# Linear layer: the two feed-forward products as three fp32r products each, and attention outputs turned into the keys' place

## The chip, the cores and the metric

The kernel runs on one core of one Trainium2 chip. The time is the device time of one execution in microseconds (us); a figure for a kernel is the median of several executions. A smaller time is better.

## The reference, cut to what matters

The program has four sublayers on an input of 8 x 1024 tokens with 256 features: softmax attention, a small linear map, a block with linear attention and a feed-forward part, and a mixture of experts. The change is in the third. What it computes (cut):

```python
x = x + _linear_attention(_layernorm(x, ln1_g, ln1_b), Wq, Wk, Wv, Wo)
h = _layernorm(x, ln2_g, ln2_b)
x = x + jax.nn.gelu(h @ Wf1, approximate=False) @ Wf2
```

`Wf1` is 256 x 1024 and `Wf2` is 1024 x 256, both in float32. These two products, over all 8192 tokens, are the feed-forward products of the title.

## The kernel before, in words

`linear_layer` walks over 16 groups of 512 tokens (8 batches, two groups each). The first group and the last are written out, and the 14 between run in a hardware loop whose body holds two. Each engine (TensorE PE, VectorE DVE, ScalarE ACT, GpSimd POOL, and SP for DMAs) has its own stream of instructions written out by hand in this order; the engines meet only at semaphores. Nothing is scheduled: what is written first on an engine runs first.

PE does in a group, in this order: queries and keys (`QK`, 16 results of 128 x 512), transposes of the keys (`KT`), the chunks of linear attention (`score`, and products into `psum_n` and `psum_u`), the transposes of its outputs (`turn_o`), the transposes of the next group's normalized input, the output product (`two_tiles` with `wo`), the next group's values (`next_v`), the transposes of the second norm's result (`turn` with `U["T2"]`), the first feed-forward product F1 (`by_feature`, L1367), and the second, F2 (`two_tiles` with `wf2`, L1377). All of these use a ring of three PSUM banks, `l_general`: a unit of work waits until the bank that it takes was emptied.

Queries, keys and values are already made in the way that the change brings to the feed-forward part: both operands are split into a high part rounded to fp32r and a low part, what is left of it, and three fp32r products (high with high, high with low, low with high) are added up in PSUM (`split_product`, L1415). The experts sublayer does the same for both of its products (L2223 and L2238). F1, F2 and the output product take plain float32 operands. A float32 matmul stands as two records in the trace, an fp32r matmul as one.

Around F1 and F2: ACT empties the two transposed tiles with scale and shift into `l_nT2` (`turned`, L1579); PE waits for both and makes F1's eight tiles of 128 features; ACT applies Gelu to each (L1645) and writes it into the place of the queries (`hT = qT`); PE waits for the last of these, then makes F2's two units, and DVE adds each to `a3` (`add_a3`, L1906). Next PE goes on to the following group's `QK`, or, behind the last group, to the remaining small steps.

Before the first group, SP loads all weights; DVE makes the high parts of `Wq`, `Wk`, `Wv` (`high_weights`, L1995 and L1999) and POOL the low parts (`low_weights`, L1728). The differences that DVE needs on the way lie in `oT`, which is not yet in use.

## Time and profile before

| | us |
|---|---|
| median of 3 runs | 4660.64 |
| lowest and highest run | 4648.56, 4662.6 |
| the profiled execution's own time | 4661.58 |
| its span in the trace | 4659.8 |

| engine | busy us | share of the span |
|---|---|---|
| PE (matmul) | 4148.9 | 89% |
| PEld (weight loads, beside PE) | 3068.7 | 66% |
| DVE | 2640.0 | 57% |
| ACT | 1911.6 | 41% |
| POOL | 1179.2 | 25% |

The shares are means over stages with different limits, so they only say where to look. The linear layer runs from about 1460 to 3700 us of the span, and PE is busy nearly all through it. A matmul's record begins when it starts and ends when its last result is out, and the next one may start before that end; the pace of a stream of matmuls is therefore read from start to start, not from the length of a record.

### The profile page before, as it was taken

How to read it: one execution, taken by the hardware profiler on the slowest of the kernel's cores; microseconds unless marked ns; L12 is line 12 of the kernel's file. 1: busy time of each engine (PE TensorE's matmuls, PEld its weight loads, DVE VectorE, ACT ScalarE, POOL GpSimd, SP SyncE). 2: the span in 40 equal slices, each digit the busy share in tenths (PEclk: the TensorE clock that was granted, in tenths of full speed). 3: DMA queues.
4: the chain of work that ended last, by engine and by line, in shares of the span. 5: the costliest groups of instructions: out<-in, count | busy, mean ns of one | idle time of the engine just before them, and what ended most of it. 6: DMA issues, size and time to landing. Idle time of an engine off the chain costs nothing. (4 is left out here: it accounts for less than half of the span.)

```text
span 4659.8 us, 76082 instructions
## 1 busy us (share of the span) xinstructions
PE 4148.9 (89%) x26100; PEld 3068.7 (66%) x26100; DVE 2640.0 (57%) x7848; ACT 1911.6 (41%) x3047; POOL 1179.2 (25%) x1094
## 2 busy tenths in 40 slices
PE   5999999999983999999999999999999499999990
PEld 2444444444432787777777877777787398989890
DVE  4787887788843455544445544444554265555554
ACT  1566666566652333333323333332333133333222
POOL 3233433334323011111111111111111123333334
PEclk8999999999976999999999999999999699999995
DMA  4443353344312000000000000000000123333335
GB/s 74 80 88 56 73 110 85 61 80 83 65 49 74 1 19 19 15 14 19 13 11 15 15 15 11 15 12 5 13 13 9 58 60 61 65 60 67 60 65 199
DMA packets 168246, 222.18 MB, mean 48 GB/s; under 512 B 26732, under 2 KB 143435, under 8 KB 167872
## 3 DMA queue, kind: packets, MB, share of 16 engines
q1 hardware_dynamic: 139840, 180.74, 16.8%
q0 software_dynamic: 25728, 28.03, 3.9%
q10 hardware_dynamic: 2304, 8.39, 0.4%
q8 instruction: 238, 3.90, 0.4%
q14 instruction: 136, 1.11, 0.1%
HBM read 85.92 MB, written 86.65 MB: 37 GB/s over the span
## 5 line engine op out<-in xcount | busy, mean ns | idle before, releaser
L787 ACT ACTIVATE probs<-a_scores 128x1024 f32<-128x1024 f32 (+3 forms) x768 | 615.8, 812 | 369.7 <-PE a_scores L691 363.1
L948 DVE CUSTOM_DVE_ANT_0 a_scores<-a_scores,mask 128x384 f32<-128x384 f32 (+3 forms) x1024 | 482.0, 515 | 119.8 <-PE a_scores L677 113.9
L1906 DVE TENSOR_TENSOR l_a<-l_general,l_a 128x512 f32<-128x512 f32 x64 | 44.3, 692 | 736.0 <-PE l_general L1377 736.0
L691 PEld LDWEIGHTS a_scores<-q_st,k_st 50*128 50x128 f32 x1536 | 150.1, 192 | 407.7 <-issue 275.6
L252 POOL TENSOR_TENSOR l_ln_rstd<-l_ln_ve,minus_half 128x4 f32<-128x4 f32 x80 | 84.1, 1051 | 1308.7 <-DVE l_ln_ve L225 1308.4
L691 PE MATMUL a_scores<-q_st,k_st 50*128 50x512 f32 (+3 forms) x1536 | 351.9, 456 | 34.2 <-issue 25.2
L951 DVE TENSOR_REDUCE mx<-a_scores 128x2 f32<-128x1024 f32 x256 | 310.7, 1223 | 110.8 <-PE a_scores L677 109.5
L711 PE MATMUL a_out<-probs,v_aug 128*32 128x512 f32 (+3 forms) x3072 | 347.6, 526 | 3.0 <-POOL probs L880 2.9
L677 PE MATMUL a_scores<-k_st,q_st 48*128 48x512 f32 (+3 forms) x1536 | 308.7, 400 | 45.6 <-ACT probs L787 27.7
L2307 POOL DMA_INDIRECT expert_sums_scratch<-e_y,e_number x136 | 220.2, 1619 | 369.0 <-DMA expert_sums_scratch<-e_y,e_number 317.0
L2238 PE MATMUL e_out<-e_weights_lo,e_hT_hi 128*128 128x256 f32 x1088 | 307.9, 283 | 0.0
L2238 PE MATMUL e_out<-e_weights_hi,e_hT_lo 128*128 128x256 f32 x1088 | 307.6, 283 | 0.0
L2238 PE MATMUL e_out<-e_weights_hi,e_hT_hi 128*128 128x256 f32 x1088 | 307.2, 282 | 0.0
L880 POOL TENSOR_SCALAR_AFFINE_SELECT probs<-probs 128x512 f32<-128x512 f32 x256 | 163.3, 639 | 560.1 <-ACT probs L787 556.6
L1517 PE MATMUL l_num<-l_v,l_scores_kept 128*128 128x65 f32 x2048 | 285.4, 262 | 0.0
L2285 ACT ACTIVATE e_to_split<-e_hidden,e_b 128x384 f32<-128x384 f32 (+1 forms) x320 | 200.0, 625 | 202.7 <-PE e_hidden L2223 197.1
L1517 PEld LDWEIGHTS l_num<-l_v,l_scores_kept 128*128 128x128 f32 x2048 | 270.3, 192 | 0.0
L1613 ACT ACTIVATE l_o<-l_general 128x512 f32<-128x512 f32 x256 | 152.9, 597 | 268.5 <-PE l_general L1415 246.1
L1367 PE MATMUL l_general<-l_nT,l_wf 128*128 128x512 f32 x512 | 225.5, 599 | 18.9 <-ACT l_nT L1579 18.9
L2223 PE MATMUL e_hidden<-e_rT_hi,e_weights_hi 128*128 128x384 f32 (+1 forms) x640 | 236.0, 369 | 0.0
L1377 PE MATMUL l_general<-l_wf,l_qT 128*128 128x256 f32 x1024 | 225.2, 381 | 11.4 <-ACT l_qT L1645 11.4
L2223 PE MATMUL e_hidden<-e_rT_lo,e_weights_hi 128*128 128x384 f32 (+1 forms) x640 | 232.6, 363 | 0.0
(243 smaller groups left out, 9538.7 us busy)
## 6 DMA issues: line engine op xcount, KB each, us to landing
q_st<-parts SPq DMA_DIRECT2D x192, 128.0 KB, 4.6
k_st<-parts SPq DMA_DIRECT2D x192, 128.0 KB, 6.3
expert_rows_scratch<-empty_row SPq DMA_DIRECT2D x8, 2210.0 KB, 14.4
e_weights<-in_L_ffn_W_dram SPq DMA_DIRECT2D x16, 1024.0 KB, 8.2
e_rows<-expert_rows_scratch SPq DMA_DIRECT2D x24, 390.0 KB
e_rows<-expert_rows_scratch SPq DMA_DIRECT2D x16, 520.0 KB
x_in<-in_L_attn_x_dram SPq DMA_DIRECT2D x8, 1024.0 KB, 6.3
expert_sums_scratch<-empty_row SPq DMA_DIRECT2D x8, 1024.0 KB, 16.4
```

Of the source, the lines that this page charges most:

```text
L677: last = nc.tensor.matmul(psum_r[:, R.slot(u), h2, 0:w], q_st[rows, 2 * hg + pair, j * P:(j + 1) * P], k_st[rows, 2 * hg + pair, k0:k1], s ...
L691: last = nc.tensor.matmul(psum_r[:, R.slot(u), h2, 0:w], k_st[rows, 2 * hg + pair, i * P:(i + 1) * P], q_st[rows, 2 * hg + pair, q0:q0 + w ...
L711: last = nc.tensor.matmul(psum_o[32 * h4:32 * h4 + 32, q0 - half * HALF:HALF], v_aug[:, i, h * DV0:h * DV0 + 32], probs[:, k % 3, h4, 0:w] ...
L787: nc.scalar.activation(probs[:, k % 3, 2 * pair:2 * pair + 2, 0:w], psum_r[:, R.slot(u), :, 0:w], ACT.Exp).then_inc(R.evacuated[R.slot(u)], 1)
L948: last = nc.vector.tensor_tensor_reduce(s, s, mask[:, HALF - w:HALF], 1.0, LEAST, ALU.add, ALU.max, out[:, h2, :])
L951: last = nc.vector.tensor_reduce(out.rearrange("p h a -> p (h a)"), psum_r[:, R.slot(u), :, 0:w], AX.X, ALU.max)
L1367: last = nc.tensor.matmul(psum_g[:, G.slot(u), :], w[:, c, cols], nT[:, c, :], start=(c == 0), stop=(c == CD - 1))
L1377: last = nc.tensor.matmul(psum_g[:, G.slot(u), jj * D:(jj + 1) * D], lhs[:, k, j * P:(j + 1) * P], rhs[:, k, :], start=(k == 0), stop=(k = ...
L1517: last = nc.tensor.matmul(psum_n[:, NUM.slot(n), h4 * DV:(h4 + 1) * DV], scores[:, d % 2, h2, p % 4, :], v_aug[:, j, 4 * g4 + h4, :], star ...
L2223: last = nc.tensor.matmul(psum_h[:, HU.slot(u), 0:n * P], w1[a][:, e2, c, m * P:(m + 1) * P], rT[b][:, q % 2, c, 0:n * P], start=(k == 0), ...
L2238: last = nc.tensor.matmul(psum_y[:, s, (j - 2 * s) * D:(j - 2 * s + 1) * D], hT[a][:, q % 2, m, j * P:(j + 1) * P], w2[b][:, e2, m, :], st ...
L2307: nc.gpsimd.indirect_dma_start(out=sums_dram, out_offset=bass.IndirectOffsetOnAxis(ap=number[:, q % RING, j:j + 1], axis=0), in_=y[:, q % ...
```

## The change

Weights. `wf1` and `wf2` become pairs of a high and a low part in fp32r. The float32 weights are loaded into the place of `kt` (`raw_f`); before the first group DVE casts both to their high parts, and POOL, behind its other low parts, subtracts to get the low ones. In the first group, ACT waits for all four before its first copy into `kt`, and PE before F1. The low parts' places also hold the differences that lay in `oT` before.

Activations. ACT writes `turned2` (the result of the second norm, turned) and `hidden` (the Gelu's results, a ring of four tiles) into the place of `kt`. DVE casts each tile to its high part and subtracts to get its low part, in the places of `l_nT2`, the queries and the keys. `oT` is no longer a tile of its own but the place of `kT`, so ACT writes the turned attention outputs where the keys were.

PE. F1's tile is six fp32r products over 512 columns (before: two float32 matmuls), F2's token tile is 24 fp32r products over 256 columns (before: eight float32 matmuls). PE waits for the high parts of the activations before F1's first product and for the low ones before its fifth; in F2, waits for hidden tile m stand in the first token tile only, one before each third product. The former waits for ACT before F1 and F2 are gone. A semaphore on POOL is merged into another.

```diff
+                def by_feature(g, u, m):
+                    cols = slice(m * P, (m + 1) * P)
                     G.wait_free(pe, g, u)
+                    terms = [(c, a, "hi") for c in range(CD) for a in ("hi", "lo")]
+                    terms += [(c, "hi", "lo") for c in range(CD)]
+                    for k, (c, a, b) in enumerate(terms):
+                        if m == 0 and k == 0:
+                            pe.wait_ge(split_hi, g * NSPLIT + CD)
+                        if m == 0 and k == 2 * CD:
+                            pe.wait_ge(split_lo, g * NSPLIT + CD)
+                        last = nc.tensor.matmul(psum_g[:, G.slot(u), :], wf1[a][:, c, cols],
+                                                nT2_parts[b][:, c, :], start=(k == 0),
+                                                stop=(k == len(terms) - 1))
+                    last.then_inc(G.full[G.slot(u)], 1)
+
+                def feed_out(g, u, i):
+                    G.wait_free(pe, g, u)
+                    for jj in range(2):
+                        j = 2 * i + jj
+                        terms = [(m, a, b) for m in range(MF)
+                                 for a, b in (("hi", "hi"), ("hi", "lo"), ("lo", "hi"))]
+                        for k, (m, a, b) in enumerate(terms):
+                            if j == 0 and k % 3 == 0:
+                                pe.wait_ge(split_lo, g * NSPLIT + CD + m + 1)
+                            last = nc.tensor.matmul(psum_g[:, G.slot(u), jj * D:(jj + 1) * D],
+                                                    hT[a][:, m, j * P:(j + 1) * P], wf2[b][:, m, :],
+                                                    start=(k == 0), stop=(k == len(terms) - 1))
+                    last.then_inc(G.full[G.slot(u)], 1)
...
-                    for c in range(CD):
-                        G.wait_evacuated(pe, g, U["T2"] + c)
+                    if first:
+                        pe.wait_ge(f_weights, 4)
                     for m in range(MF):
-                        by_feature(g, U["F1"] + m, wf1, slice(m * P, (m + 1) * P), nT2)
-                    for u in range(U["F2"] - R, U["F2"]):
-                        G.wait_evacuated(pe, g, u)
+                        by_feature(g, U["F1"] + m, m)
                     for i in range(2):
-                        two_tiles(g, U["F2"] + i, i, hT, wf2, MF)
+                        feed_out(g, U["F2"] + i, i)
...
-                    turned(g, U["T2"], nT2, 2)
+                    turned(g, U["T2"], turned2, 2)
                     for m in range(MF):
                         u = U["F1"] + m
+                        if m >= TMP:
+                            act.wait_ge(split_lo, g * NSPLIT + CD + m - TMP + 1)
                         G.wait_full(act, g, u)
-                        nc.scalar.activation(hT[:, m, :], psum_g[:, G.slot(u), :],
+                        nc.scalar.activation(hidden[:, m % TMP, :], psum_g[:, G.slot(u), :],
                                              ACT.Gelu).then_inc(G.evacuated[G.slot(u)], 1)
...
                     last.then_inc(norm2_ready, 1)
+                    for c in range(CD):
+                        G.wait_evacuated(dve, g, U["T2"] + c)
+                        nc.vector.tensor_copy(nT2_hi[:, c, :], turned2[:, c, :]).then_inc(split_hi, 1)
+                    for c in range(CD):
+                        dve.wait_ge(split_hi, g * NSPLIT + c + 1)
+                        nc.vector.tensor_tensor(nT2_parts["lo"][:, c, :], turned2[:, c, :],
+                                                nT2_hi[:, c, :].bitcast(F32),
+                                                ALU.subtract).then_inc(split_lo, 1)
+                    for m in range(MF + 1):
+                        if m < MF:
+                            G.wait_evacuated(dve, g, U["F1"] + m)
+                            nc.vector.tensor_copy(hT["hi"][:, m, :], hidden[:, m % TMP, :]
+                                                  ).then_inc(split_hi, 1)
+                        if m > 0:
+                            dve.wait_ge(split_hi, g * NSPLIT + CD + m)
+                            nc.vector.tensor_tensor(hT["lo"][:, m - 1, :], hidden[:, (m - 1) % TMP, :],
+                                                    hT["hi"][:, m - 1, :].bitcast(F32), ALU.subtract).then_inc(split_lo, 1)
                     add_a3(g, s, U["F2"])
...
+                for n, w in enumerate((wf1, wf2)):
+                    pool.wait_ge(f_weights, 2)
+                    nc.gpsimd.tensor_tensor(w["lo"][:, :, :], raw_f[n], w["hi"][:, :, :].bitcast(F32),
+                                            ALU.subtract).then_inc(f_weights, 1)
...
+                dve.wait_ge(load, 64)
+                for n, w in enumerate((wf1, wf2)):
+                    nc.vector.tensor_copy(w["hi"][:, :, :], raw_f[n]).then_inc(f_weights, 1)
```

On PE, in the loop's first group, from the transposes of the second norm's result to the first product of the next group. `l_wf1` and `l_wf2` are the weights, `l_nT2` the turned norm, `l_qT` the place of the hidden tiles, a REGISTER_ALU or ISA row sets the count of a wait. Before:

```order
L1359 MATMUL l_general<-ident,l_norm 128x128 x8
L78 REGISTER_ALU
L1367 MATMUL l_general<-l_nT2,l_wf1 128x512 x8
L72 REGISTER_ALU
L1367 MATMUL l_general<-l_nT2,l_wf1 128x512 x6
...
L78 REGISTER_ALU
L1377 MATMUL l_general<-l_wf2,l_qT 128x256 x32
L72 ISA
L1415 MATMUL l_general<-l_nT1_hi,l_w_qkv_hi 128x512
```

The same place now; each of F1's eight tiles has the six products of the first, and behind the first two groups of three that are shown, F2 has 30 more:

```order
L1379 MATMUL l_general<-ident,l_norm 128x128 x8
L1390 ISA
L1393 MATMUL l_general<-l_nT2_hi,l_wf1_hi 128x512
L1393 MATMUL l_general<-l_nT2_hi,l_wf1_lo 128x512
...
L1393 MATMUL l_general<-l_nT2_lo,l_wf1_hi 128x512 x2
...
L1407 REGISTER_ALU
L1408 MATMUL l_general<-l_wf2_hi,l_hT_hi 128x256
L1408 MATMUL l_general<-l_wf2_lo,l_hT_hi 128x256
L1408 MATMUL l_general<-l_wf2_hi,l_hT_lo 128x256
L1407 REGISTER_ALU
L1408 MATMUL l_general<-l_wf2_hi,l_hT_hi 128x256
```

F1 grew from 16 matmuls to 48 and F2 from 32 to 96, at the same place between the transposes and the next group; nothing else of PE changed its place.

On DVE, at the same place, between the second norm (L268) and the addition of F2's result. Before:

```order
L225 TENSOR_TENSOR l_ln2_ve<-l_ln2_stats 128x4
L268 TENSOR_SCALAR l_norm<-l_a3,l_ln2_mean,l_ln2_rstd 128x256 x4
L75 REGISTER_ALU
L1906 TENSOR_TENSOR l_a3<-l_general,l_a3 128x512 x2
L78 REGISTER_ALU
```

Now (`l_k` is the place where ACT leaves the tiles to be split; six more pairs of a cast and a subtraction follow the last row shown before the "..."):

```order
L268 TENSOR_SCALAR l_norm<-l_a3,l_ln2_mean,l_ln2_rstd 128x256 x4
L78 REGISTER_ALU
L2043 CAST l_nT2_hi<-l_k 128x512 x2
L2045 ISA
L2046 TENSOR_TENSOR l_nT2_lo<-l_k,l_nT2_hi 128x512
...
L2052 CAST l_hT_hi<-l_k 128x512
L78 REGISTER_ALU
L2052 CAST l_hT_hi<-l_k 128x512
L2055 REGISTER_ALU
L2056 TENSOR_TENSOR l_hT_lo<-l_k,l_hT_hi 128x512
...
L1956 TENSOR_TENSOR l_a3<-l_general,l_a3 128x512 x2
```

Twenty DVE instructions came in here in each group, ten casts and ten subtractions, all ahead of the additions; the low part of a hidden tile stands behind the high part of the next tile.

## Rows read from the trace of the kernel before

**Rows 1.** The page: busy us, share, instructions; then the granted clock in 40 slices.

```profile
PE 4148.9 (89%) x26100; PEld 3068.7 (66%) x26100; DVE 2640.0 (57%) x7848; ACT 1911.6 (41%) x3047; POOL 1179.2 (25%) x1094
...
PEclk8999999999976999999999999999999699999995
```

**Rows 2.** Windows: stretch, its us, busy of PE, PEld, DVE, ACT, POOL, clock, DMA.

```profile
1772.00:1905.00 133.00, 126.59 (x791) 104.27 (x791) 64.38 (x216) 47.86 (x81) 20.67 (x19) 1.00 0.05 17
```

**Rows 3.** Timeline of PE around F1 and F2: start us, us, instruction, idle before.

```profile
1741.87 1.03 PE L1359 MATMUL l_general<-ident,l_norm 128*128 128x128 f32 x8
1744.11 13.97 PE L1367 MATMUL l_general<-l_nT,l_wf 128*128 128x512 f32 x32 [1.20 <-ACT l_nT L1579]
1758.77 14.08 PE L1377 MATMUL l_general<-l_wf,l_qT 128*128 128x256 f32 x64 [0.69 <-ACT l_qT L1645]
1772.50 0.58 PE L1415 MATMUL l_general<-l_nT_hi,l_w_qkv_hi 128*128 128x512 f32 x1
```

**Rows 4.** F1's line, L1367: count, ns min/median/max, first and last start.

```profile
L1367 PE MATMUL l_general<-l_nT,l_wf x512: 592/592/1192, 1609.5 to 3640.8; 128*128 128x512 f32 x171
```

**Rows 5.** Timeline of PE: first, second and last of the 48 products of `next_v`.

```profile
1730.45 0.58 PE L1415 MATMUL l_general<-l_w_qkv_hi,l_nT_hi 128*128 128x512 f32 x1
1730.87 0.39 PE L1415 MATMUL l_general<-l_w_qkv_lo,l_nT_hi 128*128 128x512 f32 x1
...
1741.64 0.40 PE L1415 MATMUL l_general<-l_w_qkv_hi,l_nT_lo 128*128 128x512 f32 x1
```

**Rows 6.** Timelines of PE and PEld in the experts' second product (42 products between).

```profile
3999.81 0.28 PE L2238 MATMUL e_out<-e_weights_hi,e_hT_hi 128*128 128x256 f32 x1
...
4004.85 1.04 PE L2205 MATMUL e_turned<-ident,e_rows 128*128 128x128 f32 x8
...
3999.81 0.19 PEld L2238 LDWEIGHTS e_out<-e_weights_lo,e_hT_hi 128*128 128x128 f32 x1
```

**Rows 7.** Timelines of ACT and DVE beside F1 and F2.

```profile
1742.56 1.45 ACT L1579 ACTIVATE l_nT<-l_general,l_affine 128x512 f32<-128x512 f32 x2
...
1758.12 0.60 ACT L1645 ACTIVATE l_qT<-l_general 128x512 f32<-128x512 f32 x1 [1.12 <-PE l_general L1367]
...
1765.98 0.69 DVE L1906 TENSOR_TENSOR l_a<-l_general,l_a 128x512 f32<-128x512 f32 x1 [28.94 <-PE l_general L1377]
```

**Rows 8.** Timelines of DVE and POOL: hidden tiles split in the experts sublayer.

```profile
4027.36 0.43 DVE L2326 CAST e_hT_hi<-e_to_split 128x512 fp32r<-128x512 f32 x1 [0.86 <-ACT e_to_split L2285]
4027.70 0.69 DVE L2347 TENSOR_TENSOR e_hT_lo<-e_to_split,e_hT_hi 128x512 fp32r<-128x512 f32 x1
4028.75 0.43 DVE L2326 CAST e_hT_hi<-e_to_split 128x512 fp32r<-128x512 f32 x1 [0.36 <-ACT e_to_split L2285]
...
4030.49 2.56 DVE L2347 TENSOR_TENSOR e_hT_lo<-e_to_split,e_hT_hi 128x512 fp32r<-128x512 f32 x2
...
4030.69 1.81 POOL L2300 TENSOR_TENSOR e_y<-e_y,e_gate 128x768 f32<-128x768 f32 x1 [3.91 <-DMA expert_sums_scratch<-e_y,e_number]
```

**Rows 9.** Timeline of POOL: the next group's low parts, and its first work behind F2.

```profile
1720.53 2.49 POOL L1664 TENSOR_TENSOR l_nT_lo<-l_o,l_nT_hi 128x512 fp32r<-128x512 f32 x2 [3.60 <-DMA expert_rows_scratch<-l_rows,l_to]
...
1781.13 1.01 POOL L252 TENSOR_TENSOR l_ln_rstd<-l_ln_ve,minus_half 128x4 f32<-128x4 f32 x1 [45.20 <-DVE l_ln_ve L225]
```

**Rows 10.** Timelines of DVE, POOL, PE and ACT before and in the first group.

```profile
1492.77 2.28 DVE L1995 SCALAR_TENSOR_TENSOR l_kT<-l_kT 128x2048 f32<-128x2048 f32 x1
1495.08 6.57 DVE L1999 SCALAR_TENSOR_TENSOR l_w_qkv_hi<-l_kT 128x2048 fp32r<-128x2048 f32 x1
1501.73 4.57 POOL L1728 TENSOR_TENSOR l_w_qkv_lo<-l_kT,l_w_qkv_hi 128x2048 fp32r<-128x2048 f32 x1 [2.23 <-DVE l_w_qkv_hi L1999]
...
1506.36 0.50 PE L1415 MATMUL l_general<-l_nT_hi,l_w_qkv_hi 128*128 128x512 f32 x1 [1.69 <-POOL l_w_qkv_lo L1728]
...
1509.35 0.69 DVE L1936 SCALAR_TENSOR_TENSOR l_qT<-l_general,l_o 128x512 f32<-128x512 f32 x1 [7.70 <-ACT l_o L1617]
...
1533.04 1.56 ACT L1625 COPY l_k<-l_general 128x512 f32<-128x512 f32 x3 [2.72 <-PE l_general L1488]
```

More of the change, by code:

```diff
@@ L1165, in linear_layer, with sb_with @@
         w_qkv = {part: sb(f"l_w_qkv_{part}", [P, 3, CD, E1], F32R) for part in ("hi", "lo")}
+        def sb_with(name, shape, other_name, other_shape):
+            with nc.sbuf_tensor(other_name, other_shape, F32) as other:
+                pass
+            return sb(name, shape, F32R), other
         wo = sb("l_wo", [P, ME, D])
-        wf1 = sb("l_wf1", [P, CD, DF])
-        wf2 = sb("l_wf2", [P, MF, D])
+        wf1, wf2 = ({"hi": sb("l_wf1_hi", [P, CD, DF], F32R)}, {"hi": sb("l_wf2_hi", [P, MF, D], F32R)})
+        wf1["lo"], diff_v = sb_with("l_wf1_lo", [P, CD, DF], "l_w_v_diff", [P, NP // 2, HALF])
+        wf2["lo"], diff_q = sb_with("l_wf2_lo", [P, MF, D], "l_w_q_diff", [P, NP // 2, HALF])
         wg = sb("l_wg", [P, CD, E])
@@ L1181, in linear_layer @@
         sb("l_rows_end", [P, G4 * RW - CD * HALF])
-        nT2 = sb("l_nT2", [P, CD, HALF])
-        qT = sb("l_qT", [P, NP, HALF])
-        kT = sb("l_kT", [P, NP, HALF])
+        nT2_hi, nT2 = sb_with("l_nT2_hi", [P, CD, HALF], "l_nT2", [P, CD, HALF])
+        hT = {}
+        hT["hi"], qT = sb_with("l_hT_hi", [P, MF, HALF], "l_qT", [P, NP, HALF])
+        hT["lo"], kT = sb_with("l_hT_lo", [P, MF, HALF], "l_kT", [P, NP, HALF])
+        with nc.sbuf_tensor("l_nT2_lo", [P, CD, HALF], F32R) as nT2_lo:
+            pass
         kt = sb("l_k", [P, G4, E1])
@@ L1190, in linear_layer @@
         o = sb("l_o", [P, 2, E1])
-        oT = sb("l_oT", [P, ME, HALF])
-        hT = qT
+        oT = kT
+        flat_k = kt[:, :, :].rearrange("p j (a n) -> p (j a) n", n=HALF)
+        turned2, hidden = flat_k[:, 2:4, :], flat_k[:, 4:8, :]
+        TMP = 4
+        nT2_parts = {"hi": nT2_hi, "lo": nT2_lo}
         ex = o[:, :, :].rearrange("p s (a n) -> p (s a) n", n=HALF)
@@ L1269, in linear_layer @@
         scatter_begun = sem("l_scatter_begun")
-        rows_gone = sem("l_rows_gone")
+        f_weights = sem("l_f_weights_split")
+        split_hi, split_lo = sem("l_split_hi_ready"), sem("l_split_lo_ready")
+        NSPLIT = CD + MF
         x2_read = sem("l_x2_read")
@@ L1328, in _ @@
                                          allow_slow_non_contiguous=True).then_inc(raw_loaded[0], 16)
-                for dst, w in ((wo, Wo), (wf1, Wf1), (wf2, Wf2), (wg, Wg)):
-                    sp.dma_start(dst[:, :, :], w.rearrange("(c p) n -> p c n", p=P)).then_inc(load, 16)
+                for dst, w in ((wo[:, :, :], Wo), (raw_f[0], Wf1), (raw_f[1], Wf2), (wg[:, :, :], Wg)):
+                    sp.dma_start(dst, w.rearrange("(c p) n -> p c n", p=P)).then_inc(load, 16)
                 def store(g, s):
@@ L1620, in group @@
                         turned(g, U["T3"], nT2, None)
+                    if first:
+                        act.wait_ge(f_weights, 4)
                     for i in range(8):
@@ L1717, in group @@
                             pool.wait_ge(scattered[k], g * G4 * 16)
-                        pool.sem_inc(rows_gone, 1)
+                        pool.sem_inc(scatter_begun, 1)
                     if not last_group:
```

7 lines of the change are left out of this document (2 added, 5 removed).

## The prediction, made before the changed kernel ran

> **What bounds the kernel now.** I read the page's first part and its slices, then windows of one group of the linear layer, then the timeline of PE around the changed place, and then that of the engines which feed it. PE is busy 89% of the span, and through the linear layer at the full granted clock [rows 1]. In a group of 133.00 us PE is busy 126.59, DVE 64.38, ACT 47.86 and POOL 20.67 us, at a clock of 1.00 (2.4 GHz) [rows 2]. So PE's instruction stream sets the time, and what leaves it shortens the group if no other engine takes its place. The reader should see in the timeline that F1 begins at 1744.11, 1.20 us after the last transpose, released by ACT; F2 begins at 1758.77, after 0.69 us of waiting for the last Gelu; the next group's first product begins at 1772.50 [rows 3]. From F1's start to that product it is 28.39 us: 14.66 for F1 and the wait behind it, 13.73 for F2. F1's line has 512 records, 32 for each of 16 groups [rows 4], so this stretch comes 16 times.
>
> **PE's products.** Two of the kernel's own streams have the form of the new ones. F1's 48 products of 128 x 512 are of the form and number of the values' products: those start at 1730.45 and the next work starts at 1741.87 [rows 3, 5], 11.42 us for 48, with a slow first step (0.42 us, rows 5) in it, which F1 will have too. F2's 96 products of 128 x 256 have the form of the experts' second product: 42 of them from 3999.81 to 4004.85 [rows 6], 0.120 us each, so 11.52 us. A record of 0.28 us or a weight load of 0.19 us is longer than that pace, because they overlap [rows 6]; the pace is what PE pays. Plain float32 cost 14.66 and 13.73 with the wait; the new streams cost 11.42 and 11.52.
>
> **The wait for Gelu ahead of F2 goes.** F2 now waits tile by tile, and its first tiles were ready long before. What is late next are the last two tiles. Call F2's start S. F1's last product starts 0.23 us before S (11.42/48 = 0.24 us is the pace) and by its record of about 0.40 us [rows 5] ends at S + 0.17. Gelu takes 0.60 [rows 7], so until about S + 0.8. DVE then casts the tile (0.43, of which the next instruction waits only 0.34, from 4027.36 to 4027.70), subtracts for tile 6 and then for tile 7 (0.69 each, about 0.6 from start to start) [rows 8]: tile 6 is ready at about S + 1.9, tile 7 at S + 2.55. PE needs tile m at S + 0.36 m (three products of 0.120): S + 2.16 and S + 2.52. So F2 loses 0 to 0.1 us here. I take 0.1. Each of these waits could also slow the product behind it. The nearest price is the slow first step of a stream, 0.42 instead of 0.24 us [rows 5], about 0.19; eight of them are 1.5 us. That is the upper bound; I take none beyond the 0.1, since in the values' stream every unit has such a wait and 48 products still keep to 11.42 us with one slow step.
>
> **A longer way into F1.** ACT empties the two transposed tiles from 1742.56 to 1744.01 [rows 7], and PE began 0.10 us later. Now a cast of the second tile stands between: with 0.43 us and a semaphore's step of about 0.07, PE begins some 0.5 us later. The two low parts follow the cast at 0.34 us, and take 0.6 and 0.69; the second is ready 1.7 us after ACT's end. PE starts 0.6 after ACT's end and has four products that need no low part, 1.1 us with the slow first step, so it waits 0 to 0.1 there. Together 0.6 us. Bounds: 0.4 if the cast is all that is seen, 1.3 if both casts and both subtractions stand behind ACT's end in a row (2 x 0.43 + 2 x 0.69 = 2.24 us, less the 1.1 us of products that cover it, and the step of 0.1 to 0.2).
>
> **DVE and ACT through F1.** PE now makes a tile in 1.43 us (11.42/8). ACT needs 0.60. DVE needs a cast and a subtraction, 0.34 + 0.6 = 1.0 us, and in the experts sublayer, where it does just that at PE's pace, it sits idle 0.36 us per tile [rows 8]. DVE has 28.94 us free here [rows 7], and 20 instructions of 11 us in all fit; the additions behind them come due only when F2's first unit is done. ACT's ring of four tiles is given back by the subtraction two tiles later, well in time. What hides the split is thus that POOL is silent: in the experts, while POOL works on SBUF for 1.81 us, two subtractions take 2.56 [rows 8], 1.28 each. Here POOL has nothing to do from about 1736 to 1781 (45.20 us idle [rows 9]). The skill has the rule behind that row: the Trainium skill, "SBUF — State Buffer", section "Who interferes with whom", says that VectorE instructions with two SBUF inputs, and copies in the fast two-port mode, contend with GpSimd for one shared port pair, exclusively. By that rule the split would cost nothing in the loop and something before the first group, and both are as the rows say.
>
> **The group.** Before 28.39. After 0.6 + 11.42 + 11.52 + 0.1 = 23.64. Saved 4.75 us; 16 times, 76.0 us. With both upper bounds (1.3 and 1.5 for 0.6 and 0.1) it is 2.65 us a group, with both lower ones (0.4 and 0) 5.05: 42 to 81 us in all.
>
> **Attention outputs in the keys' place, the merged semaphore.** ACT's copies and PE's reads are the same in number, size and order; no wait is added. Zero.
>
> **Before the first group.** DVE casts two weights of 128 x 2048 behind 1501.65 (the end of its last high part), while POOL makes the last low part of `Wk` (4.57 us), which releases PE at 1506.36; DVE is next needed at 1509.35 [rows 10]. Nothing shows such a cast. Four times 0.34 is 1.4 us each, 2.7 for both, which fit the 7.70 us that DVE sits idle. But DVE's last high part took 6.57 us beside POOL's work where its neighbour without it took 2.28 [rows 10], so either of them may block the other. If the casts hold POOL up, PE starts up to 2.7 us later; if POOL holds the casts up until 1506.3, they end at 1509. I take 1 us, between 0 and 3. POOL's two new subtractions (4.6 us each, up to 6.6) end by 1523 and are wanted by ACT at 1533.04 [rows 10]: hidden by ten us of query and key products. The weights' DMAs keep their order.
>
> **The sum.** Profiled execution 4661.58 - 76.0 + 1 = 4586.6. The median of the runs is 4660.64, one us beside it; I do not correct for that. The runs lie between 4648.56 and 4662.6, so some 0.3% either way is noise, about what a measurement of this kernel can tell from no change.
>
> **The rivals.**
> *The waits inside F2 break its stream.* In the loop, each third product of the first token tile has a register instruction and a wait ahead of it, every 0.36 us, denser than any stream of products in the rows. At 0.19 us for each of eight, 1.5 us a group instead of 0.1: 22 us, so 4609. Against it stands the values' stream. It lies inside my range.
>
> *The weight loads set F2's pace, and the kernel is slower than before.* F2 goes from 64 records, each with a load, to 96. Its pace is 0.120 only if a load of 0.19 us lies beside other loads and products. If each product cost a load's 0.19 us instead, F2 would take 18.2 us, 6.7 more, and the group 30.3 instead of 28.39: 16 x 6.7 = 107, so 4694. The change loses from 0.17 us a product on ((28.39 - 0.6 - 11.42 - 0.1) / 96). Against it stand 42 products of exactly this form at 0.120 with loads of 0.19 beside them [rows 6]. The Trainium skill, "TensorE: Matmul & The Clock Gate", Part 3, "Packing small matmuls — row/col tiling", says that a weight load overlaps matmuls in flight only when their row groups differ; all these use all 128 rows. By that rule this rival would be the forecast. The trace disagrees with it, with 0.120 us between products whose loads take 0.19.
>
> *The gain is given back at a wait.* PE's next meeting with another engine could be late by as much as F2 is early, and the time stays at 4661. The one with a long chain is the low parts of the next group, behind POOL's scatter: they are ready at 1723.02 and used at 1730.45 [rows 5, 9], 7.4 us of slack, more than the 4.75 saved, and the chain starts in the same group's query stage, so it moves with PE. Little speaks for it.
>
> **How the numbers follow.** Forecast 4587, with the set-up and lead-in within their bounds, 0.82. Waits inside F2, 4609: 0.10. Weight loads, 4694: 0.04. Given back, 4661: 0.03. A mean gain larger than the bounds: 0.01. The range goes from 81 us of gain, less some noise, to beyond the second case: 4573 to 4612. Faster by over 0.3%: 0.93. Within 0.3%: 0.03. Slower: 0.04.
>
> **What would show it.** F1's products 0.23 to 0.24 us apart and F2's 0.120; from ACT's end to F1 0.6 us instead of 0.1; no wait of PE for Gelu; in F2 at most 0.1 us of waiting, at the seventh or eighth group of three; DVE idle between its pairs; a group of some 128 us. I would be wrong if F2's products stand 0.19 us apart, if F1's tiles come at DVE's pace, or if PE waits newly at the next group's low parts.

## The result and the profile after

The changed kernel takes 4605.98 us (median of 4 runs, 4591.81 to 4611.45), the kernel before 4661.62 us (4 runs, 4648.56 to 4673.35). The medians are 56 us apart. The ratio over all runs is 0.987, with a 95% interval from 0.9844 to 0.9896: 61 us less, between 48 and 73. Four more runs of the same kernel on another chip gave 4595.10 against 4661.07, a ratio of 0.9855 (0.984 to 0.9871), 66 us less by the medians. The prediction was 4587, 75 us less, with a range from 4573 to 4612. So the time lies inside the range, near its upper end, and some 10 to 20 us of the gain are missing.

The profiled execution after has 4610.1 us and a span of 4608.3. The page's busy times and granted clock after, answering to [rows 1]:

```profile
PE 4088.1 (89%) x26868; PEld 3115.5 (68%) x26868; DVE 2812.6 (61%) x8170; ACT 1910.7 (41%) x3047; POOL 1191.9 (26%) x1096
...
PEclk8899989999985999999999999999999699999995
```

PE has 61 us less to do and keeps its 89% of a shorter span; DVE has 173 us more and goes from 57 to 61%. One whole group of the loop after, from first query product to first query product (columns as in [rows 2]):

```profile
1650.71:1780.01 129.30, 123.38 (x848) 108.12 (x847) 75.39 (x236) 47.84 (x81) 21.76 (x20) 1.00 0.05 17
```

PE is still the engine without free time: 123.38 of 129.30 us. The changed place in that kernel, PE first, which answers to [rows 3] (start us, us, instruction, idle before and its releaser). Shown are the transposes, the first, second, fourth and fifth product of F1, the first two of F2, the first two of F2's eighth group of three, F2's last product and the next group's first:

```profile
1754.13 1.04 PE L1379 MATMUL l_general<-ident,l_norm 128*128 128x128 f32 x8
1756.78 0.50 PE L1393 MATMUL l_general<-l_nT_hi,l_wf_hi 128*128 128x512 f32 x1 [1.61 <-DVE l_nT_hi L2043]
1757.12 0.39 PE L1393 MATMUL l_general<-l_nT_hi,l_wf_lo 128*128 128x512 f32 x1
...
1757.58 0.40 PE L1393 MATMUL l_general<-l_nT_hi,l_wf_lo 128*128 128x512 f32 x1
1757.98 0.73 PE L1393 MATMUL l_general<-l_nT_lo,l_wf_hi 128*128 128x512 f32 x2
...
1768.39 0.28 PE L1408 MATMUL l_general<-l_wf_hi,l_hT_hi 128*128 128x256 f32 x1
1768.51 0.28 PE L1408 MATMUL l_general<-l_wf_lo,l_hT_hi 128*128 128x256 f32 x1
...
1770.91 0.39 PE L1408 MATMUL l_general<-l_wf_hi,l_hT_hi 128*128 128x256 f32 x1
1771.13 0.28 PE L1408 MATMUL l_general<-l_wf_lo,l_hT_hi 128*128 128x256 f32 x1
...
1779.90 0.28 PE L1408 MATMUL l_general<-l_wf_hi,l_hT_lo 128*128 128x256 f32 x1
1780.01 0.40 PE L1457 MATMUL l_general<-l_nT_hi,l_w_qkv_hi 128*128 128x512 f32 x1
```

DVE, ACT and PEld beside it:

```profile
1756.30 0.43 DVE L2043 CAST l_nT_hi<-l_k 128x512 fp32r<-128x512 f32 x1 [0.24 <-ACT l_k L1619]
1756.64 1.29 DVE L2046 TENSOR_TENSOR l_nT_lo<-l_k,l_nT_hi 128x512 fp32r<-128x512 f32 x2
...
1763.60 0.43 DVE L2052 CAST l_hT_hi<-l_k 128x512 fp32r<-128x512 f32 x1 [0.37 <-ACT l_k L1691]
1763.95 0.68 DVE L2056 TENSOR_TENSOR l_hT_lo<-l_k,l_hT_hi 128x512 fp32r<-128x512 f32 x1
...
1769.57 1.29 DVE L2056 TENSOR_TENSOR l_hT_lo<-l_k,l_hT_hi 128x512 fp32r<-128x512 f32 x2
...
1754.82 1.45 ACT L1619 ACTIVATE l_k<-l_general,l_affine 128x512 f32<-128x512 f32 x2
...
1768.51 0.19 PEld L1408 LDWEIGHTS l_general<-l_wf_hi,l_hT_lo 128*128 128x128 f32 x1
```

From the transposes to the next group's first query product (1780.01) it is 25.88 us; before it was 30.63 (1741.87 to 1772.50, [rows 3]). The difference is 4.75 us, to the hundredth the prediction's. What is missing lies elsewhere, and three views show where.

**First, the stages.** The table cuts each profiled span at three marks: POOL's first MEMSET of `l_keep` (end of the softmax layer), the first query product, and the first load of the experts' weights.

| us | softmax layer and setup | to first query product | linear layer | rest |
|---|---|---|---|---|
| before | 1459.90 | 46.46 | 2189.48 | 963.96 |
| before, another chip | 1470.02 | 46.53 | 2182.02 | 967.43 |
| after | 1473.34 | 47.32 | 2116.76 | 970.88 |
| after, another chip | 1457.26 | 47.38 | 2117.34 | 970.82 |

The linear layer lost 65 to 73 us, not 76. The softmax layer, which the change doesn't touch, took 13 us more than in the first row in one profiled execution of after and 3 less in the other, and 10 us more in the kernel before itself on the other chip; nothing ties it to the change.

**Second, the groups.** From one first query product to the next, the loop's groups before take 134.39 to 135.3 us (one 136.8), and 134.2 to 134.8 in the second execution. After they mostly alternate: 129.30, 131.05, 129.38, 131.32 and so on. The short ones are 5.0 shorter than before, a little more than the 4.75. The long ones are those that hold PE's loop branch, or a fall of the clock.

**Third, the waits of PE in the linear layer** (engine, line, releaser: us in total, times, longest), the first two lines from before, the two in the second block from after:

```profile
PE l_general L1367 <- ACT l_nT L1579: 18.0, 15, 1.2
PE l_general L1377 <- ACT l_qT L1645: 10.5, 15, 0.9
```

```profile
PE l_general L1393 <- DVE l_nT_hi L2043: 25.7, 16, 1.7
...
PE l_general L1457 <- issue: 9.1, 6, 1.8
```

The wait for Gelu went (10.5 us), the one ahead of F1 grew by 0.4 each, and six waits came that the prediction doesn't have. "issue" means that no semaphore event explains them. The first, with F2's last product ahead of it:

```profile
1909.33 0.28 PE L1408 MATMUL l_general<-l_wf_hi,l_hT_lo 128*128 128x256 f32 x1
1911.07 0.49 PE L1457 MATMUL l_general<-l_nT_hi,l_w_qkv_hi 128*128 128x512 f32 x1 [1.46 <-issue]
```

It stands where PE's loop jumps back, between F2's last product and the next group's first. Before, one such wait of 0.2 us is all that the view has.

The DMA queues in the trace show more of it. Queue q8 brings instructions, in packets of 16 KB, and a packet comes at each jump back, with a second one some 3 to 4 us behind it. The lines below are q8's in windows of 0.1 us in which that packet begins: packets, MB, and the time that they took as a share of 16 engines in that window (63.8% is 1.02 us). The first is from after, 1908.30 to 1908.40:

```profile
q8 instruction: 1, 0.02, 63.8%
```

The next is from before, 2174.10 to 2174.20 (91.1% is 1.46 us), with PE's first product behind that jump, the one with the wait of 0.2 us:

```profile
q8 instruction: 1, 0.02, 91.1%
```

```profile
2177.18 0.49 PE L1415 MATMUL l_general<-l_nT_hi,l_w_qkv_hi 128*128 128x512 f32 x1 [0.17 <-issue]
```

After the packet ends at 1909.37 the product starts at 1911.07, 1.69 us later; before it is 1.61 us (2175.57 to 2177.18). So it is at all 77 jumps back of PE in the thirteen executions of this document, before and after: PE's first work starts 1.5 to 1.8 us behind the end of such a packet, never earlier. The packets take 0.9 to 1.5 us, and in this execution of after the gap is longer where they do: 1.62 us from product to product with packets of 0.92 and 0.93, 2.08 with one of 1.39. What differs is when the packet begins: 2.0 to 2.6 us ahead of the last record of before's F2, 0.95 to 0.99 ahead of the last product in this execution of after. So the six waits are waits for instructions. What makes the packet begin when it does, the trace doesn't say.

### The profile page after: what moved, and what is told of

It is laid out like the page before. It is cut to its first block and busy times, and to the rows that moved or that the text cites. A ratio compares the mean times of both kernels' runs of the same rounds, so it can differ in the third digit from the quotient of the medians.

```text
span 4608.3 us, 78285 instructions
## 1 busy us (share of the span) xinstructions
PE 4088.1 (89%) x26868; PEld 3115.5 (68%) x26868; DVE 2812.6 (61%) x8170; ACT 1910.7 (41%) x3047; POOL 1191.9 (26%) x1096
## 5 line engine op out<-in xcount | busy, mean ns | idle before, releaser
L2293 PE MATMUL e_hidden<-e_rT_hi,e_weights_lo 128*128 128x384 f32 (+1 forms) x640 | 232.3, 363 | 0.0
L677 PEld LDWEIGHTS a_scores<-k_st,q_st 48*128 48x128 f32 x1536 | 157.6, 202 | 109.7 <-ACT probs L787 76.6
```

The costliest lines, as they stand in the source:

```text
L677: last = nc.tensor.matmul(psum_r[:, R.slot(u), h2, 0:w], q_st[rows, 2 * hg + pair, j * P:(j + 1) * P], k_st[rows, 2 * hg + pair, k0:k1], s ...
L2293: last = nc.tensor.matmul(psum_h[:, HU.slot(u), 0:n * P], w1[a][:, e2, c, m * P:(m + 1) * P], rT[b][:, q % 2, c, 0:n * P], start=(k == 0), ...
```

## The experiments

Each was timed against the kernel before on the same chip. Theory A says that the missing gain is chance in the other layers; it is tested by running both kernels again.

### The changed kernel and the kernel before again

> The changed kernel once more. In its first profile the stretch from the linear layer's first query product to the experts' first weight load was 72.7 us shorter than before, but the softmax layer in front of it 13.4 us longer and the experts and the end 6.9 us longer, though no line of theirs differs. Theory A, chance: these layers' length varies from one execution to the next, so the softmax layer's end (1459.9 us before, 1473.3 after) falls anywhere between about 1450 and 1480, while the linear stretch is 2117 us again within 2; over five rounds the ratio is 0.984 to 0.988, the kernel 57 to 73 us faster. Theory B, a cost of the change: the softmax layer ends at 1470 or later again, and the gain stays near 56 us, ratio 0.988.

> The kernel before, once more, for a second profile. Theory A: the linear stretch is 2189.5 us again within 2, and the softmax layer's end lies up to 15 us from 1459.9 in either direction. Theory B: the softmax layer ends within 3 us of 1459.9.

Measured: 4595.10 us (ratio 0.9855, 0.984 to 0.9871) and 4666.91 us (1.0006, 0.9994 to 1.0018). The linear layer took 2117.34 and 2182.02 us, in the table above. The linear layer of after came as expected; that of before did not, with 7.5 us less than the 2189.5 within 2 that was expected. So A explains a part, the 10 us between the two measurements (56 and 66 us less), and leaves a part: 76 us less was forecast for the linear layer, and it is 65 or 73 less, by which execution of before is taken, with six such waits at the first query product in both executions of after.

### F1 alone, and F2 alone

```diff
-                        feed_out(g, U["F2"] + i, i)
+                        two_tiles(g, U["F2"] + i, i, qT, wf2, MF)
```

(F1 alone; F2's weights and hidden tiles stay float32, and its split is not made. F2 alone is the mirror of it, with `by_feature` as before.)

> The first feed-forward product alone in three fp32r products; the second stays in plain float32, as do its weights and the hidden tiles. By the timeline of after, F1 costs 0.48 us more ahead of it and takes 11.6 us, where it took 13.97, and the wait for the last Gelu (0.69 us) is back: a gain of 1.7 to 2.0 us in each of 16 groups. Both theories: the linear stretch 27 to 33 us shorter than the 2189.5 of before. Theory A: ratio about 0.994. Theory B: less, ratio 0.997 or more.

> The second feed-forward product alone in three fp32r products; the first stays in plain float32. F1's tiles then come every 1.72 us, so the splitting has more room, the 0.69 us wait ahead of F2 goes, and F2 takes 11.6 instead of 13.73 us: a gain of 2.8 us in each group, the linear stretch 43 to 47 us shorter than 2189.5. Theory A: ratio about 0.990. Theory B: 0.993 or more. If the gains of the two parts alone do not add up to the whole, one of them hides a wait of the other.

Measured: F1 alone 4637.95 us (0.9945, 0.9932 to 0.9959), the linear layer 2156.56 us, the loop's groups 132.3 to 132.6 (two 133.9), no issue wait at the jump. F2 alone 4620.51 us (0.9901, 0.9886 to 0.9917), linear layer 2146.76, groups of 131.1 to 131.2 and of 132.5 to 133.0 in turn (two break the pattern), with this line:

```profile
PE l_general L1450 <- issue: 9.3, 6, 1.8
```

Against before's linear layer (2182 to 2189) F1's part brings 25 to 33 us and F2's 35 to 43. Both together 61 to 76, and the whole change brought 65 to 73: the parts add up. Both were expected against the 2189.5 of the first execution: F1 alone lies inside (32.9 for 27 to 33), F2 alone just under (42.7 for 43 to 47). The issue wait comes with F2's products alone.

### The turn into the keys' place alone

```diff
-        oT = sb("l_oT", [P, ME, HALF])
+        diffs = sb("l_diffs", [P, ME, HALF])
+        oT = kT
```

> The kernel before with one part of the change alone: the attention's outputs are turned into the place of the keys (l_oT is l_kT), the products of F1 and F2 stay plain fp32. As the prediction had it, this part costs nothing by itself: the keys are read last by the scores of the same group, long before the outputs are turned, and are written again by the next group's copies only after F1 has read them. Expected: groups as in the kernel before (134 to 135 us), the linear layer 2182 to 2190 us, ratio 0.998 to 1.002. Rival: the next group's key copies now wait for F1 and reach the scores late; then groups grow by over 0.5 us each and the ratio is 1.002 or more.

Measured: 4659.62 us against 4661.07, a ratio of 0.9997 (0.9987 to 1.0007), the linear layer 2183.04. The zero in the prediction holds.

### The loop's branch at another place

PE's loop is cut behind the query products, so that its branch stands there, with the same instructions in the same order.

```diff
-                groups(pe, group)
+                queries(0, units_first)
+                rest(0, 0, 0, units_first, True, False)
+                queries(1, units_group)
+                with pe.Fori(0, B - 1) as t:
+                    rest(t * 2 + 1, t, 1, units_group, False, False)
+                    queries(t * 2 + 2, units_group)
+                    rest(t * 2 + 2, t + 1, 0, units_group, False, False)
+                    queries(t * 2 + 3, units_group)
+                rest(NGR - 1, B - 1, 1, units_last, False, True)
```

> The changed kernel with PE's loop cut at another place: its body ends behind the next group's query and key products instead of behind F2; the order of PE's work and all other engines' loops stay. In after, the first product behind the branch back waits 1.5 to 1.8 us for nothing that the profile shows (six such waits, 9.1 us), and every second group takes 131.2 us where the others take 129.3; before, no such wait is seen. Theory C: while PE fetches behind its branch it lives on what is queued ahead of it, and F2's products, 0.12 us each, last half as long as plain float32 records at 0.22 us or the query products at 0.235 us. Then all groups take 129.3 to 129.6 us and the kernel is 10 to 14 us faster than the change. Theory D: it is the length of the loop's body, with 256 more records, or the branch itself: then the gap moves with the branch, and the time is that of the change within 3 us.

Measured: 4622.22 us (0.9904, 0.9887 to 0.9921), the linear layer 2135.15, 18 us more than after; 14 of them are this wait. It went from behind F2 to the place of the branch, so the branch is its place; but it grew:

```profile
PE l_general L1379 <- issue: 23.5, 6, 4.2
...
1916.36 0.39 PE L1457 MATMUL l_general<-l_nT_hi,l_w_qkv_lo 128*128 128x512 f32 x1
1920.80 1.94 PE L1379 MATMUL l_general<-ident,l_norm 128*128 128x128 f32 x8 [4.05 <-issue]
```

So the pace of the products ahead of the branch doesn't set it alone: query products stand 0.23 us apart, F2's 0.12, and the gap behind the slower ones is the longer one. That falls outside what was expected. What is different there is that the query products wait for their banks from unit to unit. So theory L: PE gets at what lies behind the branch only while no wait ahead of the branch is open; this takes some 5 us in all; what dense work stands between the last wait and the branch hides so much of it.

The packets bear half of this out. In this kernel they moved with PE's branch, though no other engine's stream changed. The packet begins only 1.3 to 1.9 us behind the start of the last product, and the first transpose follows its end by 1.6 to 1.8 us as elsewhere. But L with its 5 us does not fit after itself: in the group shown above F2's last open wait ends at 1770.9, 9.1 us before the next group begins, and F2 passes just so in the groups with the gap. Where no wait is open, the packet begins less far ahead of the last product when the products are denser: 0.4 to 1.0 us with F2's, which are 0.12 apart, 2.0 to 2.6 with plain float32 records, which are 0.22 apart. That is theory C. So the trace speaks for C where no wait is open and for L where one is; neither is shown by itself.

### The branch behind the output product, and the wait ahead of F1 filled

The next two take away as well PE's longest wait that comes in every group: the last two of the eight pieces of the next group's values are made between the transposes and F1, where PE waited 1.61 us for ACT and DVE.

```diff
                     if not last_group:
-                        next_v(g, g + 1, U)
+                        next_v(g, g + 1, U, range(VA))
                     pe.wait_ge(norm2_ready, g + 1)
                     turn(g, U["T2"], norm)
+                    if not last_group:
+                        next_v(g, g + 1, U, range(VA, 8))
```

> The changed kernel with the transposes of the second norm ahead of the last two of the eight value products' units on PE (and the same order on ACT), so that ACT's emptying, the casts and the subtractions lie beside 2.8 us of products. PE waits 1.61 us ahead of F1 and 0.17 us before its fifth product in each group of the change. If this wait is all that the way into F1 costs, 15 groups (the last has no value products) gain 1.7 to 1.8 us each, 25 to 27 us in all against the change; the group is 127.5 us. The rival: the norm's result comes later than the sixth unit ends, PE waits there for DVE instead, and the gain is under 10 us.

Measured: 4565.56 us (0.9779, 0.9763 to 0.9795), the linear layer 2089.33, 27 to 28 less than after, where 25 to 27 were expected. PE's transposes, values and F1 now stand without a gap; F1 takes 11.25 us instead of 11.61, since neither its slow first step nor the wait at its fifth product is left. The groups are 127.5 to 128.1 and 129.3 to 129.7 us in turn, with the issue wait as in after.

The second of the two has in addition the branch behind the output product, a stream of plain float32 matmuls (`attend` ends there and `feed` begins with the values):

```diff
+                attend(1, 0, 1, units_group, False, False)
+                with pe.Fori(0, B - 2) as t:
+                    feed(t * 2 + 1, t, 1, units_group, False, False)
+                    attend(t * 2 + 2, t + 1, 0, units_group, False, False)
+                    feed(t * 2 + 2, t + 1, 0, units_group, False, False)
+                    attend(t * 2 + 3, t + 1, 1, units_group, False, False)
```

> The kernel with the keys' part of the turned queries (DMA, last transpose group) brought forward as in early_turn, and TensorE's loop cut at another place: its branch stands behind the output product of the attention of a group, ahead of F1, and not behind F2. The instructions and their order are otherwise early_turn's. What it tells apart is where the gap of 1.5 to 1.8 us comes from, which stood behind the branch after F2 in every second group, and grew to 4.2 us when the branch was put behind the query products. Theory L (TensorE fetches past a branch only when nothing ahead of it still waits on a semaphore; the fetch takes some 5 us and is hidden where more work than that stands behind the last wait ahead of the branch): the output product waits for nothing after its first products, so the gap shrinks to nothing or moves under the wait that opens F1; all groups take 127.3 to 127.9 us, the linear layer is 12 us shorter than in early_turn (2077 against 2089), the time 10 to 14 us under early_turn. Theory F (the gap is the price of a branch that stands between dense products, wherever it is put): a gap of 1.5 us or more is seen at the first product behind the branch in each of the 7 passes, and groups alternate as in early_turn (127.5 and 129.4). Theory R (what follows the branch sets it: only where the product behind it also waits for a semaphore is it seen): no gap, but then early_turn's group behind the loop, too, should have had none.

> The same kernel as early_turn, beside the one with the moved branch on the same chip, so that the two can be set against each other. Every theory: the linear layer 2089 us within 3, groups of 127.5 and 129.4 us in turn, a gap of 1.5 to 1.8 us behind the branch in each of six or seven passes; the time 0.976 to 0.980 of the kernel before.

(What early_turn brings forward is the transposes of the second norm, as in its diff, and the loop of the moved branch jumps back five times.)

Measured side by side: 4551.84 us (0.9757, 0.9744 to 0.977) with the branch moved, 4574.00 (0.9801, 0.9787 to 0.9814) without. The groups are 127.2 to 127.7 us (one 129.1) instead of 127.3 and 129.0 in turn (one 130.6); the linear layer takes 2077.57 us, against 2084.55 in this pair and 2089.33 in the first execution. So of the 22 us between the medians the moved branch accounts for 7 to 12; the profiled executions have most of the others in the softmax layer (1451.45 against 1468.10), which both kernels share. The kernel beside it missed what was expected of it: its linear layer is 4.5 us shorter than 2089, its ratio is 0.9801 for at most 0.980, and its gaps are 1.3 to 1.7 us for 1.5 to 1.8. PE's issue waits of each, the moved one first:

```profile
PE l_general L1458 <- issue: 0.7, 4, 0.2
```

```profile
PE l_general L1458 <- issue: 8.5, 6, 1.7
```

So a branch between dense products is not dear by itself (theory F falls): behind 14 us of plain float32 matmuls it costs 0.2 us of idle time at most. The kernel before had it behind just such products, those of its F2, which is why its trace has no such wait. The packets come 2.1 to 2.6 us ahead of the last record here too, as in before, and the first product 1.7 us behind their end. L foretold the short gap, but so does C, and R asks for none either; how far ahead PE reads, and whether it counts in time or in instructions, no run here settles. This is the fastest kernel of the study.

### A later F2, and a slower split

Do the waits inside F2 bring what the prediction's first rival feared, if they become real? Once PE waits for all eight hidden tiles ahead of F2; once DVE makes each subtraction twice (the added one comes first and writes into `norm`, which is free then).

```diff
-                            if j == 0 and k % 3 == 0:
-                                pe.wait_ge(split_lo, g * NSPLIT + CD + m + 1)
+                            if j == 0 and k == 0:
+                                pe.wait_ge(split_lo, g * NSPLIT + CD + MF)
```

> The changed kernel with one wait ahead of F2 for all eight tiles' low parts instead of one wait ahead of each tile's products. In the trace of after the last low part is ready 2.45 us behind F2's start and costs 0.10 us there. If the waits tile by tile are what hides the split, the group is 2.2 to 2.5 us longer, 35 to 40 us in all against the change. If the eight waits themselves cost something (the second case of the prediction, 0.19 us each), that part is won back and the loss is under 20 us.

```diff
                             dve.wait_ge(split_hi, g * NSPLIT + CD + m)
+                            nc.vector.tensor_tensor(norm[:, m % 2 * 2:m % 2 * 2 + 2, :].rearrange("p a n -> p (a n)"), hidden[:, (m - 1) % TMP, :],
+                                                    hT["hi"][:, m - 1, :].bitcast(F32), ALU.subtract)
```

> The changed kernel with each hidden tile's subtraction done twice, the first into a place that nothing reads. DVE's work on a tile goes from 0.96 to 1.58 us, PE's stays at 1.41 us a tile. If DVE has the slack that the trace shows (0.38 us idle a tile), only what goes beyond it shows, at the end of F2's first token tile: 1.0 to 1.5 us a group, 15 to 25 us in all against the change. If the split were on the path already, each subtraction would show in full: 8 x 0.6 us x 16, 75 us or more.

Measured: 4655.13 us (0.9966, 0.9951 to 0.9982) and 4649.21 us (0.9962, 0.9947 to 0.9977). Both lose more than the theories gave (35 to 40, and 15 to 25), 57 and 53 us of the linear layer against after. The waits themselves are, the first line from the first kernel, the second from the second:

```profile
PE l_general L1408 <- DVE l_hT_lo L2056: 35.4, 15, 2.5
...
PE l_general L1408 <- DVE l_hT_lo L2058: 22.3, 30, 0.9
```

That is 2.36 us of idle time a group in the first, where 2.2 to 2.5 were expected, and 1.5 in the second, where 1.0 to 1.5 were; from start to start, F1 with the wait behind it is 2.5 us longer in the first (14.11 for 11.61) and F2 2.0 us longer in the second (13.50 for 11.50 between its first and last product). But most groups grew by more, the first kernel's by 4.4 where they hold no branch. The rest is mainly in the clock. Windows of the first kernel (idle time, then F2's first products, then the next ones):

```profile
1761.00:1764.00 3.00, 0.65 (x4) 0.21 (x2) 2.57 (x5) 0.60 (x1) 0.00 (x0) 1.00 0.00 0
1764.00:1767.00 3.00, 3.00 (x15) 3.00 (x16) 0.00 (x0) 0.00 (x0) 0.00 (x0) 0.55 0.00 0
1767.00:1770.00 3.00, 3.00 (x25) 3.00 (x24) 0.00 (x0) 0.00 (x0) 0.00 (x0) 0.88 0.02 5
```

Behind the wait the granted clock is 0.55 of full speed, between the two levels and close to the lower one, 1.2 GHz, for some 3 us: 15 products where 25 fit. F2 takes 12.99 us there between its first and last product, 1.5 more than the 11.50 of after. With the 2.5 it makes 4.0 of the 4.4. But the same wait does not always bring it: of the fourteen groups behind the first and ahead of the last, nine have the slower F2, two have F1 slower by as much, and three (the tenth, fourteenth and fifteenth) have neither. The second kernel shows 0.65 and 0.78 in the 6 us behind a wait of 0.58, with an F2 of 14.98 for 13.50, and again 1.5 us lost. So, the last group aside, each fall of the clock in F1 or F2 cost 1.5 us, behind the short wait as behind the long one.

## Why the prediction was right, and what it missed

**PE's pace.** Right. F1's products stand 0.23 to 0.24 us apart, its 48 take 11.61 us with the wait at the fifth (11.42 and 0 to 0.1 foretold); F2's 96, from 1768.39 to 1780.01, take 11.62 (11.52 + 0.1 foretold). The loads take 0.19 us each and still stand beside products 0.12 apart, so the rival in which they set the pace fell. The rule that the prediction gave with it (the Trainium skill, "TensorE: Matmul & The Clock Gate", Part 3, "Packing small matmuls — row/col tiling") is not what these rows show: there the load is said to overlap only where the row groups differ, here all use the same rows and the pace is 0.12 us.

**The wait ahead of F2.** Right: none for Gelu. The last low part is ready at 1770.86 (1769.57 and 1.29), 2.47 after S = 1768.39, where 2.55 was worked out; the one lost step is at the eighth group of three, 0.22 instead of 0.12. The seven other waits cost nothing (22 products in a row 0.12 apart), so the rival of the broken stream fell too: a wait that is already met is free here.

**The way into F1.** Right. 0.6 foretold, 0.5 for the cast and 0.1 at the low parts. From ACT's end (1756.27) to the first product it is 0.51 instead of 0.10, so 0.41 for the cast, the same by which the wait grew (from 1.20 [rows 3] to 1.61); and 0.17 at the fifth product (0.40 instead of 0.23). Together 0.58. With F1 and F2 the group's sum is 0.41 + 11.61 + 11.62 = 23.64, as forecast. (The group of some 128 us that was to be seen came from a window of 133.00 us [rows 2], which is not a whole group: from first query product to first query product it was 134.4 and more, and 129.3 is what follows.)

**DVE.** Right. It has 0.32 to 0.44 us idle per tile from the third on, with a cast of 0.43 and a subtraction of 0.68, as in the experts' rows [rows 8]. POOL runs nothing between 1748.2 and 1785 in that group, as the prediction had it; that the lengths come from POOL's silence is argued from the rows, since no run here puts POOL to work beside F1.

**Before the first group.** 1 us foretold, 0.9 measured (46.46 to 47.32). The mechanism is the bound's: of casts and POOL's low part, one holds up the other. The first cast takes 1.22 us; POOL's last low part begins 0.16 behind its start and takes 5.44 us where it was 4.57 [rows 10], 0.87 more, and releases PE. The second cast takes 5.54 us, until 1.1 behind POOL's end. Together the casts stand as 6.68 us:

```profile
1515.01 6.68 DVE L2078 CAST l_wf_hi<-l_k 128x2048 fp32r<-128x2048 f32 x2
...
1515.17 5.44 POOL L1774 TENSOR_TENSOR l_w_qkv_lo<-l_kT,l_w_qkv_hi 128x2048 fp32r<-128x2048 f32 x1 [2.23 <-DVE l_w_qkv_hi L2066]
...
1520.66 0.50 PE L1457 MATMUL l_general<-l_nT_hi,l_w_qkv_hi 128*128 128x512 f32 x1 [3.24 <-POOL l_w_qkv_lo L1774]
```

**What the sum lacked.** The step that failed is "The group ... 16 times": a term is missing from six of them. Where PE's loop jumps back, the gap between two products is 1.62 to 2.08 us instead of 0.12; the six of this execution make 10.0 us (in the second execution 10.6). The prediction looked at what PE does in the first of the loop's two groups only, and at the last product of F2 as if the next stood behind it in a straight line. A second, smaller term is the clock: in two of the first 15 groups of either execution F1 takes 13.0 to 13.2 us instead of 11.61, and the clock in it is low, as in the sixth group here:

```profile
2279.00:2281.00 2.00, 2.00 (x6) 1.57 (x6) 0.33 (x2) 0.60 (x1) 0.00 (x0) 0.61 0.00 0
2281.00:2283.00 2.00, 2.00 (x6) 1.52 (x6) 0.14 (x1) 0.36 (x1) 0.00 (x0) 0.53 0.00 0
```

On the other side, a group without either is 5.0 us shorter and not 4.75; the 0.3 lie between the query products and the transposes (103.42 to 103.50 instead of 103.77 us in every second group; with F1 alone 103.5 to 103.6), and no run says why. In sum: 76 less 10 to 10.6 for the branch and less 3 for the clock gives 62 to 63. The linear layers of the two executions of after are 65 us shorter than that of the second execution of before. Against its first execution it is 73, but that one is itself 7.5 us longer than the second, nearly all of it between the query products and the transposes, where the change touches nothing and where after takes as long as the second. Of the 10 us between the two measurements (56 and 66), a part could be chance in the other layers: in the profiled execution of the first one the softmax layer took 1473.34 us where that of before had 1459.90, and the last part 970.88 against 963.96. Each measurement's interval holds the other's ratio.

**The range** held by luck: its upper half was meant for another case (waits inside F2, 4609), which did not come, and a gap of about the same weight did. With the branch's 10 us in the sum the forecast would have been 4597.

## What to carry to other kernels

Read the place where a hardware loop jumps back as a term of its own: when the products ahead of the branch become denser, a gap behind it can appear that the trace of before doesn't show. Look at the instruction queue's packets there. Put the branch behind slow records without open waits; here that alone was worth 7 to 12 us. Where a stream has both the operands' preparation and a wait at its head, move independent products into the wait: 27 to 28 us came from doing the 1.0 us of transposes ahead of twelve products of each group instead of behind them. A wait of PE costs more than its length when the clock falls behind it, here 1.5 us for each fall in F1 or F2.

## What was not expected of the hardware

- The gap behind PE's loop branch (idle time): 1.3 to 1.9 us behind fp32r products of 128 x 256 that are 0.12 us apart, 3.6 to 4.2 behind query products that wait for their banks, 0 to 0.2 behind 14 us of plain float32 matmuls. PE's first work behind the branch started 1.5 to 1.8 us after the end of a 16 KB packet of instructions, at all 77 jumps.
- The granted clock: 0.55 for 3 us behind a wait of 2.36 us (0.50 in another group), and nothing of the kind behind the same wait in three groups of fourteen; 0.65 and 0.78 behind one of 0.58 on top of an earlier one of 0.92; yet behind the 1.61 us ahead of F1 F1 keeps its full pace in 13 of the first 15 groups of either execution. A fall in F1 or F2 cost 1.5 us each time, the last group aside. What sets one apart from the other stays open.
- Seven more waits on semaphores within 3 us of products cost nothing where they are already met.
- The length of the softmax layer, whose code is the same in all kernels here, lay between 1451.45 and 1473.34 us from execution to execution, a spread of 22 us, a third of this change's gain.
